# Scan matrix as 32x32 blocks, scan products in four row groups, and work moved between VectorE, GpSimd and ScalarE

## The reference, cut to what matters

```python
proj = einsum('bld,pd->blp', hidden_states, in_proj_w)      # gate, hbc, dt
xBC  = silu(causal_conv4(hbc) + conv_bias)                  # x, B, C
dt_p = softplus(dt + dt_bias); A = -exp(A_log)
# per head: state = state*exp(dt_p*A) + (dt_p*x) B^T ; y_t = state C_t
y  = scan + x * D
yg = y.reshape(B, L, 8, 512)
yn = yg * rsqrt(mean(yg*yg) + eps) * norm_weight * silu(gate)
out = einsum('bli,di->bld', yn, out_proj_w)
```

## Time and profile before

| | us |
|---|---|
| median of 3 runs (3389.19 to 3389.84) | 3389.36 |
| the profiled execution, its own time | 3390.82 |
| its span, from first to last instruction | 3389.1 |

### The profile page before, as it was taken

How to read it: one execution, slowest core, us unless ns; L and a number is a source line. 1 busy time by engine, 2 the same in 40 slices (tenths; PEclk the granted TensorE clock), 3 DMA queues, 4 the chain that set the end, 5 groups by cost and what they waited for, 6 DMA issues and landing times. The chain is left out here.

```text
span 3389.1 us, 58506 instructions
## 1 busy us (share of the span) xinstructions
PE 3367.0 (99%) x19482; PEld 2838.5 (84%) x19482; DVE 3010.4 (89%) x4815; ACT 1495.0 (44%) x2691; POOL 444.9 (13%) x328
## 2 busy tenths in 40 slices
PE   8999999999999999999999999999999999999999
PEld 6788888888888888888888888888888888888888
DVE  6899999999999999999999999999999999998443
ACT  5655554444444444444444444444444444443111
POOL 1111111011110111101111011110111110111333
PEclk9999999999999999999999999999999999999999
DMA  7433363334433353335433362335433352225331
GB/s 271 169 123 110 113 232 127 118 126 165 167 125 117 130 193 135 126 115 190 137 132 130 112 223 108 127 133 185 146 111 124 137 181 92 84 89 155 93 93 59
DMA packets 207789, 466.23 MB, mean 138 GB/s; under 512 B 35134, under 2 KB 80606, under 8 KB 198284
## 3 DMA queue, kind: packets, MB, share of 16 engines
q1 hardware_dynamic: 206364, 464.72, 39.1%
q0 software_dynamic: 368, 0.85, 0.1%
q10 hardware_dynamic: 1024, 0.27, 0.0%
HBM read 313.68 MB, written 152.09 MB: 137 GB/s over the span
## 5 line engine op out<-in xcount | busy, mean ns | idle before, releaser
L1121 PE MATMUL p_cv<-ht,wt 128*128 128x512 f32 x5376 | 1274.2, 392 | 0.8 <-DVE xc L1349 0.8
L1121 PEld LDWEIGHTS p_cv<-ht,wt 128*128 128x128 f32 x5376 | 1003.9, 188 | 224.1 <-issue 11.0
L1212 PE MATMUL bank<-wot,gy 128*128 128x512 f32 x3072 | 727.0, 392 | 0.0
L1212 PEld LDWEIGHTS bank<-wot,gy 128*128 128x128 f32 x3072 | 571.9, 188 | 119.6 <-DVE y L1399 0.2
L1349 DVE SCALAR_TENSOR_TENSOR xc<-p_cv,cvw,xc 128x496 f32<-128x496 f32 (+2 forms) x768 | 544.3, 716 | 18.3 <-ACT xc L1253 0.2
L1121 PE MATMUL bank<-ht,wt 128*128 128x512 f32 x2304 | 554.4, 389 | 0.0
L1121 PEld LDWEIGHTS bank<-ht,wt 128*128 128x128 f32 x2304 | 431.9, 188 | 89.3
L1253 ACT ACTIVATE xc<-p_cv,cvb,cvw 128x512 f32<-128x512 f32 x256 | 199.7, 781 | 452.2 <-PE p_cv L1121 452.2
L1073 POOL TENSOR_TENSOR r<-rv,neg_half 128x4 f32<-128x4 f32 x64 | 88.8, 1388 | 2317.2 <-DVE rv L1429 2317.2
L1235 ACT ACTIVATE xc<-xc 128x512 f32<-128x512 f32 x384 | 236.0, 630 | 151.1 <-DVE xc L1349 145.2
L1067 POOL TENSOR_TENSOR segr<-adts,mask_le 128x1024 fp32r<-128x1024 f32 x128 | 242.8, 1918 | 425.9 <-DVE adts L1332 425.9
(11 more groups left out here) (193 smaller groups left out, 3583.7 us busy)
## 6 DMA issues: line engine op xcount, KB each, us to landing
ht<-h_d SPq DMA_DIRECT2D x63, 2048.0 KB, 7.8
acc_d<-acc SPq DMA_DIRECT2D x64, 1024.0 KB, 4.3
wt_d<-wnext SPq DMA_DIRECT2D x112, 512.0 KB, 3.4
acc<-acc_d SPq DMA_DIRECT2D x56, 1024.0 KB, 7.0
wt<-wt_d SPq DMA_DIRECT2D x70, 512.0 KB, 8.2
stage<-in_L_attn_in_proj_w SPq DMA_DIRECT2D x84, 256.0 KB, 2.7
wot<-wt_d SPq DMA_DIRECT2D x28, 512.0 KB, 6.6
xb<-in_x SPq DMA_DIRECT2D x8, 1024.0 KB, 7.6
```

The lines of the kernel that those rows point to most:

```text
L1121: ins = pe.matmul(pb[:, :], wt[:, n, l, k, :], ht[:, rr, k, :], start=(q == 0 and k == 0), stop=(q == 2 and k == KC - 1))
L1212: ins = pe.matmul(bank[OUT[t]][:, :], gy[:, c, l, t * P:(t + 1) * P], wot[:, rr, c, :], start=(c == 0 and q == 0), stop=(c == CT - 1 and q ...
```

## The change

The diff below is cut: declarations of semaphores, the two extra GpSimd loops (which now run over g and j) and the renaming of PSUM banks 0 to 3 into one tensor `low_banks` in stages 2 and 3 are left out.

```diff
-PROJ_BANK = (0, 1, 2, 0, 1, 2, 0, 1, 2, 0)
+PROJ_BANK = (0, 1, 2, 0, 1, 2, 0, 1, 2, 4)
-    m = ... "m", [P, HG, TT, P]
+    m = ... "m", [P, TT, HG, L]
+    step_of = ... "step_of", [P, TT, HG, L]
-    XT, SEG, CB, YB, OUT, SSQ, NEXT = (3, 4, 5, 7), (5, 7), 6, (6, 7, 4, 5), (2, 3, 4, 5), 6, (0, 1)
+    XT, SEG, CB, OUT, SSQ, NEXT = (4, 5, 6, 7), (4, 5), 3, (5, 6, 7, 4), 3, (5, 6)
 # GpSimd, after the two products of L1067
+            pool.wait_ge(s_m, SEGB * it + SEGB)
+            pool.tensor_tensor(step_of, dt of the block, broadcast over l, sh.mask_le, ALU.mult)   # s_step
+        def decay_products(g, j):
+            for q in range(SEGB):
+                pool.wait_ge(s_exp, SEGB * it + q + 1)
+                pool.tensor_tensor(decay[:, tiles], decay[:, tiles], step_of[:, tiles], ALU.mult)    # s_stepped
 # TensorE
-                        ins = pe.matmul(bank[YB[c]][u * HP:(u + 1) * HP, t * P:(t + 1) * P], dtx[:, t, h * HP:(h + 1) * HP],
-                                        m[:, h, t, :], start=True, stop=True)
-                ins.then_inc(s_yp, 1)
+                        for b in range(BT):
+                            rows = slice(b * L, (b + 1) * L)
+                            ins = pe.matmul(scanned[u * HP:(u + 1) * HP, b, (c * TT + t) * L:(c * TT + t + 1) * L],
+                                            dtx[rows, t, h * HP:(h + 1) * HP], m[rows, t, h, :], start=True, stop=True)
-                ins = pe.matmul(bank[CB][:, t * P:(t + 1) * P], xc[:, 0, t * P:(t + 1) * P], xc[:, 1, t * P:(t + 1) * P], ...)
+                for b in range(BT):
+                    cols = slice(t * P + b * L, t * P + (b + 1) * L)
+                    ins = pe.matmul(bank[CB][b * L:(b + 1) * L, t * L:(t + 1) * L], xc[:, 0, cols], xc[:, 1, cols], ...)
-            for c in range(CT - 1 if prepare else CT - 2):
+            for c in range(CT - 2):
 ...  turn_x ...
+            pe.wait_ge(s_conv, NCV * it + NCV)
+            project(NCV + CT - 2)
             for u in range(2 if prepare else 0):       # turning of the next weights
-                pe.wait_ge(s_z, CT * it + CT + 1 + u)
+                pe.wait_ge(s_dtx, TT * it + 2 + u)
-            pe.wait_ge(s_cbm, it + 1)
-            pe.wait_ge(s_exp, SEGB * it + SEGB)
+            pe.wait_ge(s_m, SEGB * it + 2 * SEGB)
+            pe.wait_ge(s_dtx, TT * it + TT)
+            pe.wait_ge(s_z, CT * it + CT + 3)
             for c in range(CT):
-                scan(c)
+                ins = scan(c)
+            ins.then_inc(s_yp, 1)
             project(NCV + CT - 1)
 # ScalarE
+            for t in range(TT):                        # behind gate(1)
+                act.wait_ge(s_xt, TT * it + t + 1)
+                act.activation(dtx[:, t, :], bank[XT[t]][:, :], ACT.Copy).then_inc(s_dtx, 1)
+            skip(0); skip(1)                           # xc[2 + c] = xc[2 + c] * D, in place
             gate(2)
 ...  high halves of the next weights ...
+            skip(2); skip(3)
 # VectorE
-            spread_cb(), four scan_matrix(t), four times_dt(t)
+            for q in range(SEGB):                      # waits for s_cb and s_stepped
+                dve.tensor_tensor(m[:, tiles], products of bank[CB], broadcast over heads, decay[:, tiles], ALU.mult)  # s_m
+            join(1, la, lb, 5) ... all joins and pairs that stood among and behind add_squares ... copy_predicated
             low halves of the next weights (L1387)
             for c in range(CT):
-                dve.wait_ge(s_yp, CT * it + c + 1)
-                dve.scalar_tensor_tensor(y[:, c, :], xc[:, 2 + c, :], dsk[:, c:c + 1], bank[YB[c]][:, :], ALU.mult, ALU.add)
+                if c == 0: dve.wait_ge(s_yp, it + 1)
+                dve.wait_ge(s_skip, CT * it + c + 1)
+                dve.tensor_tensor(by_residue(y[:, c, :]), by_residue(xc[:, 2 + c, :]), scanned[:, :, c * P:(c + 1) * P], ALU.add)
```

More of the change, by code:

```diff
@@ L1085, in gpsimd_part @@
         pool.wait_ge(sh.s_mask, 4)
+        decay_products(0, 0)
         root(0)
@@ L1101, in gpsimd_part, with scan_pass @@
             pool.wait_ge(sh.s_cbq, spread)
+            decay_products(0, 1 + s)
             root(1 + s)
[L1103 to L1106, removed]
+        def scan_pass(g, j):
+            scan_products(g, j)
+            decay_products(g, j)
+            root(NBLK * g + j)
+        with pool.Fori(1 + R, NBLK) as j:
+            scan_pass(0, j)
+        with pool.Fori(1, G - 1) as g:
+            with pool.Fori(0, NBLK) as j:
+                scan_pass(g, j)
+        with pool.Fori(0, NBLK - 1) as j:
+            scan_pass(G - 1, j)
+        scan_products(G - 1, NBLK - 1)
+        decay_products(G - 1, NBLK - 1)
         pool.wait_ge(s_proj, NPJ * (NIT - 1) + 7)
@@ L1239, in gate, with skip @@
                 act.activation(z[:, c, :], bank[PROJ_BANK[NCV + c]][:, :], ACT.Silu).then_inc(s_z, 1)
+            def skip(c):
+                act.activation(xc[:, 2 + c, :], xc[:, 2 + c, :], ACT.Copy, scale=dsk[:, c:c + 1]).then_inc(s_skip, 1)
             def high(c):
@@ L1270, in attend @@
                 act.activation(wnext[:, u, 0, :], bank[NEXT[u]][:, :], ACT.Copy).then_inc(s_nhi, 1)
+            skip(2)
+            skip(3)
             high(0)
@@ L1362, in attend, with scan_matrix @@
                     find_here(0)
[L1364 to L1374, removed]
-                                  bank[XT[t]][:, :].rearrange("p (h c) -> p h c", h=HG),
-                                  sh.dt[:, ds(TT * j + t, 1), ds(HG * g, HG)].rearrange("p o h -> p (o h)").unsqueeze(2).to_broadcast([P, HG, HP]),
-                                  ALU.mult).then_inc(s_dtx, 1)
-            dve.wait_ge(s_cbm, it + 1)
-            for t in range(TT):
-                scan_matrix(t)
-            for t in range(TT):
-                times_dt(t)
+            def scan_matrix(q):
+                tiles = slice(q * TT // SEGB, (q + 1) * TT // SEGB)
+                if q == 0:
+                    dve.wait_ge(s_cb, it + 1)
+                dve.wait_ge(s_stepped, SEGB * it + q + 1)
+                products = bank[CB][:, 0:TT * L].rearrange("p (t l) -> p t l", t=TT)
+                dve.tensor_tensor(m[:, tiles, :, :], products[:, tiles, :].unsqueeze(2).to_broadcast([P, TT // SEGB, HG, L]),
+                                  decay[:, tiles, :, :], ALU.mult).then_inc(s_m, 1)
+            for q in range(SEGB):
+                scan_matrix(q)
+            join(1, la, lb, 5)
+            join(1, lc, ld)
+            pair(4, lb, 6)
+            pair(5, ld, 7)
+            join(2, la, lc)
+            join(1, lb, ld, 9)
+            pair(6, lc, 10)
+            pair(7, ld, 11)
+            join(1, lc, ld, 13)
+            join(2, lb, lc, 14)
+            join(3, la, lb, 15)
+            w8_step(16)
+            dve.sem_inc(s_w8go, 1)
+            dve.copy_predicated(sh.w8[:, wt_tile, :], here[:, :], la).then_inc(s_w8, 1)
             for u in range(2 if prepare else 0):
@@ L1405, in attend, with add_squares @@
                     low(c - 1)
-            def add_squares(c, done):
+            def add_squares(c):
                 dve.wait_ge(s_sq, CT * it + c + 1)
@@ L1478, in mix_and_attend @@
     with ExitStack() as ctx:
-        sh.bank = sh.p_cv + [ctx.enter_context(nc.psum_tensor(f"bank{n}", [P, 512], F32)) for n in range(2, 8)]
+        sh.bank = [sh.low_banks[:, n, :] for n in range(BT)] + [ctx.enter_context(nc.psum_tensor(f"bank{n}", [P, 512], F32)) for n in range(BT, 8)]
         opens, attends = attend_part(nc, a, sh, ctx)
@@ L1550, in stage3 @@
         p_cv = sh.p_cv
-        p_ss = [ctx.enter_context(nc.psum_tensor(f"p_ss{u}", [P, 512], F32)) for u in range(2)]
+        p_ss = [sh.low_banks[:, 2 + u, :] for u in range(2)]
         p_y = [[ctx.enter_context(nc.psum_tensor(f"p_y{u}{q}", [P, 512], F32)) for q in range(2)] for u in range(2)]
@@ L1826, in build @@
         sh.s_cv = sem("conv2_done")
-        sh.p_cv = [ctx.enter_context(nc.psum_tensor(f"p_cv{u}", [P, 512], F32)) for u in range(2)]
+        sh.low_banks = ctx.enter_context(nc.psum_tensor("low_banks", [P, BT, 512], F32))
+        sh.p_cv = [sh.low_banks[:, u, :] for u in range(2)]
         def at_top(name, shape, offset, dt=F32):
```

95 lines of the change are left out of this document (42 added, 53 removed).

## The result

The kernel after takes 3439.56 us (median of 4 runs, 3437.28 to 3441.43) against 3389.6: ratio 1.0147, 95% interval 1.0134 to 1.0159. It is slower by 1.5%; 3368 was forecast, with slower at 0.40. Lines L1155 (projections), L1162, L1172 (scan), L1191 (C.B), L1219, L1243 (output products) are PE's; L1351 `pair`, L1359 `join`, L1363 `find_here`, L1405 scan matrix, L1427 low halves of the weights, L1432 `low`, L1444 y, L1449 z are DVE's; L1087 is GpSimd's decay product.

What follows compares the result with a forecast made beforehand. PE, busy 99%, was taken as the bound, with DVE's chain deciding the output products' start after the change: 56 x -0.4 + 8 x 0.2 = -21, 3390.8 - 21 = 3370, 1.5 less for the median: 3368 us, range 3335 to 3485.

Steps and rivals of the forecast that it cites:

- Scan products: PE's scan: 256 short passes on eight tiles side by side take 2.0 us instead of 3.64, at 0.062 us a step.
- A: Rival, chance 0.18: PE's small passes run in one line, scan 7.7 us, +5.6 us an iteration, 3753 us in all.
- B: Rival, chance 0.17: only four of PE's eight tiles work at a time, scan 4.0 us, +1.3 us an iteration, 3480 us.
- the sign turns at 2.7 us: Gain becomes loss once PE's scan passes take over 2.7 us, with y(0) after 1552.73.
- C.B products: PE's 32 passes on four column groups take 0.73 us instead of about 0.89, a gain of 0.16.
- Order on PE: Third gate projection moves behind turning x, no PE time; its gate is covered except in the last group.
- DVE's chain: DVE's path through search, low halves and y to the first output product sets its start: 1556.0 against 1556.42, -0.4 us.
- D: Case counted to the forecast's 0.50: POOL products at 0.96 us shorten the path to y, PE decides everywhere, 3352 us.
- Rival C: Chance 0.15: DVE's path to the output products is longer, POOL at 1.56 adds 0.5 us, 3397; each further 0.1 adds 6.
- The sum: Output products start 0.4 us earlier in 56 iterations and 0.2 later in the last group's 8: -21 us together.
- Costed at nothing: Changed DVE, ACT and POOL work, later output quarters, row sums and DMAs were taken as covered by slack, 0 us.
- Range: Whole kernel's time from 3335 to 3485 us, leaving out the 3753 us case; the forecast's own range is 3340 to 3385.

Runs made afterwards that it cites:

- early_pairs: The kernel after, with `find_here` and pairs 0 to 3 one tap earlier on DVE, away from GpSimd's decay products; 3395.77 us, 1.0018 of before.
- before_search_ahead: The kernel before, with only the table search moved ahead of the low halves of the next weights and y; 3873.63 us, 1.1427 of before.

## Why the prediction was wrong, step by step

- **Scan products.** Forecast 2.0 us, measured 2.67; A's 7.7 and B's 4.0 are out. The step of a tile was right (0.062 forecast, 0.061 with four tiles). Missing was what holds eight tiles to 83 ns a step, 10.4 ns a pass over all tiles; no row of before could show it. By the prediction's own account the sign turns at 2.7 us, so this term alone takes away what the scan was to bring.
- **C.B products.** Forecast gain 0.16, measured 0.42.
- **Order on PE.** As forecast; in the last group the scan waits for its gate with 0.69 us of idle.
- **DVE's chain**, the step that failed: it took DVE's instructions at their length in the kernel before, and reckoned nothing for two of them running beside GpSimd's new products. Forecast 18.6 us from the sixth projection's ACT tap to the output products, measured 1581.31 - 1561.66 = 19.65. Right were the search (7.90 for 7.8), the low halves (1.19 for 1.21) and the stretch from y(0) (3.65 for 3.69). The decay products were 2.74 us for two instead of 2.60; their own size was right, since in early_pairs, with nothing of that kind beside them, the mean is 1.30 us as forecast (1.39 here). What the chain left out is that DVE's `pair(3)` and `find_here` grow beside them, and GpSimd's second product too. Without DVE's growth the second scan matrix step would end its input wait with GpSimd at 1567.17 and the search start at 1567.85; it starts at 1568.57. That is 0.72 us, and handing over and GpSimd's longer products together 0.29. With 0.13 for the search and the 0.06 won behind it, 1.08 us an iteration. early_pairs gave 0.78 back. D (shorter) didn't come. Rival C had the right place (each 0.1 us adds 6: 1.08 x 56 = 60) but priced only GpSimd's own length.
- **The sum.** Per iteration, -0.4 was +0.69 (55 iterations), +0.2 was +0.53. Even without the contention the change would have brought next to nothing: then the scan's true 2.67 us decides, and in early_pairs' trace 23 of the first 55 iterations are 0.2 us shorter than before and 32 are 0.03 shorter, the last group's 0.5 longer. The two first passes (8 us) put early_pairs 6 us over before.
- **Costed at nothing.** The taps, skips and squares were covered. Not seen were the two first passes, 7.8 us with the 0.8 that the chain has everywhere: GpSimd, SP and ACT were asked for cover, PE's instruction stream was not, though its count rose from 19482 to 33306.
- **Range.** 3439.6 lies in 3335 to 3485, which rival B's price had stretched for another reason.

## What to carry to other kernels

When work moves to GpSimd, ask which DVE instructions run beside it, and move those to a stretch where DVE waits anyway; a longer mean of an unchanged instruction is the sign to look for. When several signals become one, everything behind it comes later: each consumer's order (here low(0), then ACT's gate) has to be drawn up again, and each repair shows the next wait. Try a repair on the schedule it is meant for: the same edit gave 44 us and cost 82.

## What was not expected of the hardware

```profile
q8 instruction: 1, 0.02, 0.6%
...
q8 instruction: 3, 0.05, 1.6%
```
  Each is 16 KB. In the kernel after the first of the three starts 1.2 us behind the scan's start and has landed at 142.62, and PE goes on 1.4 us later. All eleven kernels whose scan stops have such a packet in both of their first passes, and PE goes on 1.2 to 1.5 us behind its landing; between 151 and 2801 us the kernel after has none on q8. The Trainium skill, "Runtime: NRT & Kernel Launch", Instruction fetch mechanics, says that code comes in blocks of 16 KiB and that this is hidden behind issue, a taken branch to code outside of the window apart; the trace has the blocks, but a stop of 1.9 us in the middle of a loop's body isn't hidden. That PE waits for them rests on the times agreeing; no run changes the code's place.
- **The clock falls in a scan on two tiles**, though PE is never idle in it: 1.00 in its first 2.2 us, 0.50 in its last 3.6. It was at 0.50 behind the 5.2 us of idle in before_search_ahead and behind the stop of 1.89 us in the kernel after, and a projection then took 5.1 to 5.3 us for 2.9. Idle of that length doesn't always bring it: in early_pairs it stayed at 1.00 behind 1.99 us.
```profile
145.53 1.19 PE L1172 MATMUL low_banks<-m,dtx 32*64 32x32 f32 x99 [1.99 <-issue]
146.65 3.01 PE L1155 MATMUL bank<-ht,wt 128*128 128x512 f32 x12
```
